# Decoder layer stack, L0 cross-attention: the head-pair loop on TensorE written out, and both copies of the odd head's turned integers on ScalarE

## Time and profile before

| | |
|---|---|
| median of 3 runs | 4089.97 us (4089.8 to 4091.74) |
| profiled execution | 4092.45 us, span of the core 4090.7 us |
| busy over the span | PE 85%, DVE 54%, ACT 41%, POOL 14% |
| the changed stage | about 1353 to 2428 us of the span |
| mean granted TensorE clock | 0.917 of full speed |

### The profile page before, as it was taken

One profiled execution on the slowest core, in us unless ns is written; L12 is line 12 of the kernel. 1 busy time (PEld: TensorE's weight loads), 2 busy tenths in 40 slices (PEclk: granted clock), 3 DMA queues, 4 the chain that ended last, 5 costly groups with the idle time before them and its releaser, 6 DMA issues. The chain is left out here.

```text
span 4090.7 us, 65484 instructions
## 1 busy us (share of the span) xinstructions
PE 3475.5 (85%) x20492; PEld 2246.0 (55%) x20492; DVE 2221.5 (54%) x4572; ACT 1677.6 (41%) x3311; POOL 565.4 (14%) x326
## 2 busy tenths in 40 slices
PE   4898998989857578888888878989995888999998
PEld 2565656556544345555555544557773555555554
DVE  4545555464528888888888873235552444222222
ACT  1333333343326577777777751124442333111110
POOL 2222323122230000000000000023331222000000
PEclk8999999999979799999999987989997888999999
DMA  3000000000000000000000010000004000000000
GB/s 113 1 0 0 0 0 0 0 0 0 0 10 19 0 0 0 0 0 0 0 0 0 0 34 0 0 11 0 0 0 122 7 6 3 1 0 0 0 0 21
DMA packets 33660, 35.54 MB, mean 9 GB/s; under 512 B 2924, under 2 KB 32080, under 8 KB 32848
## 3 DMA queue, kind: packets, MB, share of 16 engines
q10 hardware_dynamic: 17360, 19.22, 1.4%
q1 hardware_dynamic: 16256, 15.77, 1.3%
HBM read 32.83 MB, written 2.10 MB: 9 GB/s over the span
## 5 line engine op out<-in xcount | busy, mean ns | idle before, releaser
L1309 ACT ACTIVATE x_ints<-x_p_s,x_nb,x_sq 128x1024 uint16<-128x1024 f32 x512 | 611.8, 1199 | 176.0 <-DVE x_nb L1340 163.3
L1219 PE MATMUL x_p_s<-x_kT,x_qz 128*128 (+1 forms) x1024 | 340.5, 418 | 154.0 <-ACT x_ints L1309 133.2
L1244 PE MATMUL x_p_t<-identb,x_ints 128*128 128x128 bf16 x4096 | 345.1, 233 | 53.3 <-DVE x_turned L1349 34.8
L2094 DVE TENSOR_TENSOR f_h<-f_act_g,f_p_u 128x512 f32<-128x512 f32 (+1 forms) x132 | 90.8, 688 | 550.1 <-PE f_p_y L1989 480.6
L1336 DVE TENSOR_SCALAR_CACHE_REDUCE x_passed<-x_p_s,x_hmax 128x1024 bf16<-128x1024 f32 x256 | 328.1, 1281 | 75.8 <-PE x_p_s L1219 73.7
L1244 PEld LDWEIGHTS x_p_t<-identb,x_ints 128*128 128x128 bf16 x4096 | 264.0, 104 | 168.8 <-issue 113.1
L1327 DVE TENSOR_REDUCE x_hmax<-x_p_s 128x1 f32<-128x1024 f32 x256 | 313.5, 1225 | 54.7 <-issue 35.6
L1254 PEld LDWEIGHTS x_p_o<-x_vi,x_turned 128*128 128x128 f16 x4096 | 256.9, 98 | 127.1 <-issue 39.8
L2039 ACT ACTIVATE f_act_g<-f_p_g 128x512 f32<-128x512 f32 (+1 forms) x132 | 78.3, 597 | 578.2 <-PE f_p_g L1974 578.1
L1254 PE MATMUL x_p_o<-x_vi,x_turned 128*128 (+1 forms) x4096 | 306.3, 175 | 1.0 <-DVE x_turned L1349 0.9
L1974 PE MATMUL f_p_g<-f_xT,f_wg 128*128 128x512 f32 (+1 forms) x528 | 271.4, 638 | 15.4 <-ACT f_xT L2026 10.1
(11 more groups left out here) (336 smaller groups left out, 6322.1 us busy)
## 6 DMA issues: line engine op xcount, KB each, us to landing
f_wg<-in_L_ffn_w_dram ACTq DMA_DIRECT2D x2, 1408.0 KB, 9.4
f_wu<-in_L_ffn_w_dram ACTq DMA_DIRECT2D x2, 1408.0 KB, 10.3
f_wd<-in_L_ffn_w_dram ACTq DMA_DIRECT2D x1, 2816.0 KB, 11.7
x_res<-in_x_dram SPq DMA_DIRECT2D x1, 2048.0 KB, 8.8
a_wq<-in_L_attn_Wq_dram ACTq DMA_DIRECT2D x1, 2048.0 KB, 7.6
a_wk<-in_L_attn_Wlk_dram ACTq DMA_DIRECT2D x1, 2048.0 KB, 11.9
a_wv<-in_L_attn_Wlv_dram ACTq DMA_DIRECT2D x1, 2048.0 KB, 16.3
a_wo<-in_L_attn_Wo_dram ACTq DMA_DIRECT2D x1, 2048.0 KB, 21.6
```

The lines of the kernel that those rows point to most:

```text
L1219: return pe.matmul(p_s[half][par][:, c * BANK:(c + 1) * BANK], qz[:, par, :, :, :].rearrange("p a b t -> p (a b) t")[:, bass.ds(n, 1), :]. ...
L1244: mm = pe.transpose(p_t[:, c * P:(c + 1) * P], ints[par][:, half, c * P:(c + 1) * P].bitcast(BF16), core.identb[:, :])
L1309: act.activation(ints[par][:, half, :], p_s[half][par][:, :], ACT.Exp, bias=nb[:, par:par + 1], scale=of_pass(sq[:, par, :, :].rearrange(" ...
L2094: i = dve.tensor_tensor(h[n % 2][0:m, :], act_g[n % 2][0:m, :], p_u[n % 2][0:m, :], ALU.mult)
```

## The change

On TensorE the loop over pairs is written out: all eight pairs have their own code, with `a` a number, and only the loop over the query blocks inside a pair stays. The addresses of kT and vi no longer come from a register.

The copy of half 0 of the odd head moves from VectorE to ScalarE. ScalarE's order in a pass is now: copy of half 1 of the last pass's odd head, exponentials of the even head, copy of half 0 of the last pass's odd head, copy of half 1 of the even head, exponentials of the odd head. VectorE keeps only the copy of half 0 of the even head. TensorE's waits follow: turning half 1 of the even head waits for ScalarE's third count of the pass before instead of VectorE's copy.

```diff
-        t_act = count("t_act", 2)
-        t_dve = count("t_dve", 2)
+        t_act = count("t_act", 3)
+        t_dve = count("t_dve", 1)
...
-                          kT[:, bass.ds(a, 1), half * HALF + c * BANK:half * HALF + (c + 1) * BANK].rearrange("p a n -> p (a n)"),
+                          kT[:, a, half * HALF + c * BANK:half * HALF + (c + 1) * BANK],
...
                 if half:
                     pe.wait_ge(e_up.sem, e_up.of(n, 2 * par + 1))
-                    pe.wait_ge(t_dve.sem, t_dve.of(n, 1) if par else t_dve.of(n - 1))
+                    if par:
+                        pe.wait_ge(t_dve.sem, t_dve.of(n))
+                    else:
+                        pe.wait_ge(t_act.sem, t_act.of(n - 1, 3))
...
-                pe.wait_ge(t_act.sem, t_act.of(n, par + 1))
-                pe.wait_ge(t_dve.sem, t_dve.of(n, par + 1))
+                pe.wait_ge(t_act.sem, t_act.of(n, 3 if par else 1))
+                if not par:
+                    pe.wait_ge(t_dve.sem, t_dve.of(n))
                 for k in range(B):
                     mm = pe.matmul(p_o[:, par * XD:(par + 1) * XD], turned[par][:, k, :].bitcast(F16),
-                                   vi[:, k, bass.ds(a * (2 * XD) + par * XD, XD)], start=(k == 0), stop=(k == B - 1))
+                                   vi[:, k, (2 * a + par) * XD:(2 * a + par + 1) * XD], start=(k == 0), stop=(k == B - 1))
...
-            with pe.Fori(2, B) as t:
-                emit((0, t), (0, t - 1), (0, t - 2))
-            with pe.Fori(1, PAIRS) as a:
+            for a in range(PAIRS):
                 n = a * B
-                emit((a, n), (a - 1, n - 1), (a - 1, n - 2))
-                emit((a, n + 1), (a, n), (a - 1, n - 1))
+                if a:
+                    emit((a, n), (a - 1, n - 1), (a - 1, n - 2))
+                    emit((a, n + 1), (a, n), (a - 1, n - 1))
                 with pe.Fori(2, B) as t:
-                    emit((a, n + t), (a, n + t - 1), (a, n + t - 2))
+                    emit((a, t + n), (a, t + (n - 1)), (a, t + (n - 2)))
...
-            def leave(par):
+            def leave(par, half):
                 def run(n):
-                    act.wait_ge(t_made.sem, t_made.of(n, 2 * par + 1))
+                    act.wait_ge(t_made.sem, t_made.of(n, 2 * par + 2 - half))
                     act.wait_ge(o_made.sem, o_made.of(n - 1, par + 1))
-                    act.copy(turned[par][:, 8:16, :].rearrange("p k n -> p (k n)").bitcast(I32),
+                    act.copy(turned[par][:, 8 * half:8 * half + 8, :].rearrange("p k n -> p (k n)").bitcast(I32),
                              p_t[:, :].bitcast(I32)).then_inc(t_act.sem, 1)
...
-            pipeline(act, [("leave1", 1), ("exp0", 0), ("leave0", 0), ("exp1", 0)],
-                     {"leave1": leave(1), "exp0": exps(0), "leave0": leave(0), "exp1": exps(1)}, PASSES)
+            pipeline(act, [("leave11", 1), ("exp0", 0), ("leave10", 1), ("leave01", 0), ("exp1", 0)],
+                     {"leave11": leave(1, 1), "exp0": exps(0), "leave10": leave(1, 0), "leave01": leave(0, 1),
+                      "exp1": exps(1)}, PASSES)
...
             pipeline(dve, [("max0", 0), ("leave0", 1), ("keep", 2), ("row0", 0),
-                           ("max1", 0), ("leave1", 1), ("row1", 0)],
+                           ("max1", 0), ("row1", 0)],
```

More of the change, by code:

```diff
@@ L1343, in row_max, with leave @@
                 return run
[L1345 to L1350, removed]
+            def leave(n):
+                dve.wait_ge(t_made.sem, t_made.of(n, 2))
+                dve.wait_ge(o_made.sem, o_made.of(n - 1, 1))
+                dve.tensor_copy(turned[0][:, 0:8, :].rearrange("p k n -> p (k n)"), p_t[:, :].bitcast(U16)).then_inc(t_dve.sem, 1)
             def keep(n):
@@ L1356, in _ @@
             pipeline(dve, [("max0", 0), ("leave0", 1), ("keep", 2), ("row0", 0),
-                           ("max1", 0), ("leave1", 1), ("row1", 0)],
+                           ("max1", 0), ("row1", 0)],
                      {"max0": half_max(0), "max1": half_max(1), "row0": row_max(0), "row1": row_max(1),
-                      "leave0": leave(0), "leave1": leave(1), "keep": keep}, PASSES)
+                      "leave0": leave, "keep": keep}, PASSES)
 def x0_output(core, sv, att, esum, ahead):
```

## The result

The changed kernel takes 4115.26 us (median of 5 runs, 4110.42 to 4121.39) against 4089.97 us before: a ratio of 1.0055, 95% interval 1.0038 to 1.0073. It is slower, by 0.4 to 0.7%, and inside the predicted range. The profiled execution took 4117.14 us against 4092.45.

The account below looks back on a forecast made before the run. It took the stage to be bound by a loop of waits through the shared score buffer, no engine being full. 4092.45 + 16.5 (legs) + 10 (clock) = 4119 us profiled, less 2.5 for undisturbed runs: 4117 us, range 4102 to 4150.

Parts of the forecast that it names:

- 16.5 for the full-clock legs: All 255 legs: 1082.2 us predicted, including 0.8 for the first slow ones, which is 16.5 above 1065.70.
- The sum is 2.39 + 0.58 + 0.14 + 0.61 + 0.12 + 0.58: ScalarE's two exponentials, copy, handover, TensorE's eight turnings, handover, copy up to the odd exponential: 4.42 us, taken as 4.44.
- Leg A: From the even head's first exponential to the odd head's; predicted to grow by 0.28, from 4.16 to 4.44 us.
- A pass is 4.44 + 4.04 = 8.48 against 8.35: One pass, both heads of a pair, at the full clock: predicted 8.48 us after the change, 8.35 before.
- The copy costs more than the written-out pair gives: Claim for a full-clock pass: moving the copy to ScalarE outweighs writing out TensorE's pair loop, 8.48 us against 8.35.
- leg B: From the odd head's first exponential to the next even one; predicted to go from 4.19 to 4.04 us.
- The clock term of 10 us: TensorE's lower clock slows turnings now in the ScalarE chain: 20 passes x (0.42 + 0.10) = 10 us; bounds 0 and 56.
- at the same share: Step assuming TensorE stays at the lower clock for 16% of the stage as before, so 20 of 128 passes are slow.
- the fall as a rival with 18%: TensorE's clock drops to its lower level in about half of the passes, adding 56 us: 4160 us; chance 18%.
- The written-out pair at 16.8 us: TensorE's value group shortens without the register step, saving 0.15 us in about 112 odd-to-even legs: 16.8 us.
- The seven further code starts at 0: Seven more pieces of TensorE code run for the first time; taken as 0, upper bound 29 us.
- VectorE's copy at 0: Removing VectorE's copy of the odd head's turned half, made while it waits for scores: worth 0.

Follow-up runs that it names:

- after_shortcopy2: The changed kernel with ScalarE's copy of the odd head's half 0 cut to 4 of 8 blocks, outputs not the reference's; 4106.07 us, one run.
- after_filler4: The changed kernel plus four unread 480-column matmuls a pass, two ahead of the odd head's scores and two behind; 4081.39 us, 0.9955 to 0.9982 of the kernel before.
- unroll_only: The kernel before with only TensorE's pair loop written out, VectorE keeping its second copy; 4076.48 us, 0.9951 to 0.9975 of the kernel before.
- static_all: The kernel before with TensorE's pair loop and the loop over query blocks written out, copies unmoved; 4064.47 us, 0.9920 to 0.9947 of the kernel before.

## Why the prediction was right, and where it was not

- **Direction and size.** 4117 us was forecast, 4115.26 measured. That the sum is so near is luck: two wrong terms nearly cancel. Over the 1065.70 us of legs before, I had 16.5 for the full-clock legs and 10 for the clock, together 26.5. Measured are -9.6 and 32.3, together 22.7.
- **"The sum is 2.39 + 0.58 + 0.14 + 0.61 + 0.12 + 0.58".** Leg A did become this chain, as after_shortcopy2 shows. Its size was 4.23, not 4.44. Measured: 2.38, 0.58, 0.05, 0.62, 0.12, 0.48. Two handovers were misread. The 0.14 was taken from the last pass, which is written-out code, and the loop has 0.05. The 0.58 from copy to exponential was taken from the earlier trace rows, where the exponential did not wait for the copy but for the bias (the bias step at 1489.08, below, plus the 0.44 that lies between the two in the earlier trace rows, is 1489.52): a coincidence. Here an exponential starts 0.48 after the start of a copy, 0.11 before the copy's recorded end.
  The bias step ahead of the earlier trace rows, from the timeline of the kernel before:

```profile
1489.08 0.21 DVE L1340 TENSOR_SCALAR x_nb<-x_top,x_nsq 128x1 f32<-128x1 f32 x1
```

- **"A pass is 4.44 + 4.04 = 8.48 against 8.35".** It failed with that: at the full clock a pass is 8.28, and after_filler4's legs take 1056.07 us where I had 1082.2. "The copy costs more than the written-out pair gives" is wrong at the full clock, where by the estimate above the two are level. The 8.35 was too high as well: I took 4.19 for every leg B behind pair 0, but of the 72 of those 111 that ran at the full clock only 39 took it, and 19 took 4.04 or 4.05.
- **The clock term of 10 us.** It measured 32.3. The step that failed is "at the same share", and with it the price of a slow pass, 0.42 for the turning and 0.10 for late scores. The granted clock fell from 0.92 to 0.89, and the turning in leg A is the smaller part, 10.3 us. The larger part, 22.0, is in legs B, where the score matmuls met the low clock in 46 legs against 9 before, at 0.43 each. In the earlier trace rows they paced leg B already; why the low clock now falls on them so often is not shown. I had the fall as a rival with 18% and priced it by half of all passes slow in both legs, 56 us; 24 legs A and 46 legs B were slow. (That rival's 4160 takes the 2.5 us off twice; its sum is 4162.) The rule of the Trainium skill on long waits (TensorE: Matmul & The Clock Gate, section "HAM oscillation — how this bites in real kernels") would have left this term at 0. The trace does not agree: the clock fell with no wait of the matmuls above 1.5 us between the first and the last of these legs, and filling part of the waits held it.
- **Leg B of 4.04.** Right: 4.05 at the full clock.
- **The written-out pair at 16.8 us.** Near, at 15.6, but in part by luck: legs B gave 10.2, since not all of them had been 4.19, and legs A the rest. The seven further code starts at 0: nearly right; in after_filler4 15 seam legs A are 4.31, 0.08 more each.
- **VectorE's copy at 0.** Right: the row maximum of leg A at 1861.25 waits 1.28 us for TensorE, against 0.69 in the earlier trace rows.

## What to carry to other kernels

Read a handover between two engines only from a row in which the second engine surely waited for the first, and in the same kind of code (loop or written out) as the place that it is used for. When a change puts a TensorE group that had slack into the loop that sets the pace, price the lower clock with it, and test that by matmuls that nobody reads in the idle time. A chain that looks like the cost can be the smaller part. Here the longer leg A (4.23 against 4.16) and the gain of the written-out pair were level at the full clock, and the whole loss of 22.7 us is about what the lower clock cost more than before (32.3 against an estimated 10).

## What the runs showed of the hardware

- Extra work made the kernel faster: four matmuls of 480 columns a pass raised the granted clock of the stage from 0.89 to 1.00 and took 32.3 us off the legs (1088.40 to 1056.07); the medians are 4115.26 and 4081.39.
- TensorE started the turning 0.05 to 0.06 us after ScalarE's copy in the loop and 0.14 us after it in written-out code, both at the full clock (after_filler4).
- Sixteen value matmuls took 2.00 us with their address in a register and 0.55 us with a constant one (230 of the 256 groups of unroll_only).
- The scores behind an exponential start 1.45 us after its start where they head the loop's body (leg A), and 1.35 both further down in the loop (leg B) and in written-out code (static_all).
- ScalarE started an exponential 0.48 us after the start of a copy of 0.59 us (the change, 1862.74 and 1863.22).
- TensorE ran 128 passes of written-out code (static_all) with the scores 1.35 us behind the exponential in every leg, so without a wait for instructions there.
